# Gathering the tokens' expert rows in two rounds, with four additions placed in the last up projection

## The reference, cut to what matters

```python
def moe(x, gate_w, w1, w3, w2):            # x: 1024 x 512, E = 8, F = 1024, TOPK = 2
    logits = x @ gate_w
    topv, topi = top_k(logits, 2)
    probs = softmax(topv)
    for e in range(8):
        g = silu(x @ w1[e]) * (x @ w3[e])
        out += w[:, e:e + 1] * (g @ w2[e])   # w: probs at the token's two experts, else 0
    return out

out = h + moe(rmsnorm(h), ...)
x = layernorm(x + out)
```

## Time and profile before

| | |
|---|---|
| timed runs, us | 1427.38, 1428.01, 1431.57 |
| profiled execution, us | 1442.2 |
| its span, first to last instruction | 1440.6 |
| mean granted clock of TensorE | 0.965 |
| PE busy | 1318.8 us, 92% |
| DVE busy | 1023.2 us, 71% |
| ACT busy | 808.7 us, 56% |
| POOL busy | 366.7 us, 25% |

### The profile page before, as it was taken

One profiled execution on the slowest core, in us unless ns is written; L12 is line 12 of the kernel. 1 busy time (PEld: TensorE's weight loads), 2 busy tenths in 40 slices (PEclk: granted clock), 3 DMA queues, 4 the chain that ended last, 5 costly groups with the idle time before them and its releaser, 6 DMA issues. The chain is left out here.

```text
span 1440.6 us, 24551 instructions
## 1 busy us (share of the span) xinstructions
PE 1318.8 (92%) x7925; PEld 713.0 (49%) x7925; DVE 1023.2 (71%) x1966; ACT 808.7 (56%) x1460; POOL 366.7 (25%) x602
## 2 busy tenths in 40 slices
PE   7988999999999999998688999999959999999974
PEld 4444444444444444443344555555436556666751
DVE  5847777777777777777567887888768556666736
ACT  5447666666666666666336575665734444555422
POOL 5402020202010101104256365664326000000042
PEclk9999999999999999999798999999979999999987
DMA  8327776666665767587453453535595866677641
GB/s 250 60 59 133 148 116 136 122 128 139 115 144 112 153 116 150 106 182 132 154 158 72 87 118 60 142 64 102 100 235 184 297 171 188 212 225 239 232 125 60
DMA packets 451868, 206.18 MB, mean 143 GB/s; under 512 B 401088, under 2 KB 415424, under 8 KB 451776
## 3 DMA queue, kind: packets, MB, share of 16 engines
q1 hardware_dynamic: 448640, 196.67, 58.1%
q0 software_dynamic: 2560, 8.39, 1.8%
q10 hardware_dynamic: 576, 0.00, 0.0%
HBM read 87.38 MB, written 16.45 MB: 72 GB/s over the span
## 5 line engine op out<-in xcount | busy, mean ns | idle before, releaser
L1539 DVE SCALAR_TENSOR_TENSOR X<-xa_SC,xa_rs,X 128x1024 f16<-128x1024 f32 x128 | 164.4, 1284 | 98.5 <-issue 97.8
L1347 ACT ACTIVATE X<-xa_SC,xa_rs 128x1024 f16<-128x1024 f32 x128 | 147.1, 1149 | 110.7 <-POOL xa_rs L1044 110.7
L1220 PE MATMUL xa_psS<-xa_KT,xa_QT 128*128 128x512 f16 x768 | 186.4, 379 | 6.1 <-DVE xa_mn L1572 4.7
L1232 PE MATMUL xa_psO<-wide,xa_V 128*128 128x512 f16 x768 | 173.3, 383 | 7.1 <-DMA wide<-X 7.0
L1044 POOL TENSOR_SCALAR xa_rs<-xa_rc,flag 128x1 f32<-128x1 f32 x128 | 34.2, 267 | 516.2 <-DVE xa_rc L1532 516.2
L1572 DVE CUSTOM_DVE_ANT_0 xa_SC<-xa_psS,maskb 128x1024 f32<-128x1024 f32 x128 | 155.1, 1211 | 4.5 <-PE xa_psS L1220 2.4
L1369 ACT ACTIVATE xa_SC<-xa_SC,xa_mn 128x1024 f32<-128x1024 f32 x128 | 145.4, 1136 | 13.4 <-DVE xa_mn L1572 13.3
L1232 PEld LDWEIGHTS xa_psO<-wide,xa_V 128*128 128x128 f16 x768 | 74.5, 98 | 102.1 <-issue 16.9
L1220 PEld LDWEIGHTS xa_psS<-xa_KT,xa_QT 128*128 128x128 f16 x768 | 73.4, 98 | 90.7 <-DVE xa_mn L1572 9.4
L1369 ACT ACTIVATE sa_SC<-sa_SC,sa_mn 128x128 f32<-128x128 f32 (+3 forms) x128 | 71.5, 559 | 78.2 <-DVE sa_mn L1572 78.0
L2065 PE MATMUL rmoe_psU<-rmoe_XGT,W 128*128 128x352 f16 (+6 forms) x768 | 109.4, 291 | 3.8 <-issue 3.8
(11 more groups left out here) (295 smaller groups left out, 2251.5 us busy)
## 6 DMA issues: line engine op xcount, KB each, us to landing
first<-in_L_ffn_w_dram SPq DMA_DIRECT2D x12, 2048.0 KB
W2raw<-in_L_ffn_w_dram SPq DMA_DIRECT2D x8, 2048.0 KB, 9.0
expert_rows_dram<-zeros SPq DMA_DIRECT2D x10, 512.0 KB, 9.5
xa_WPraw<-in_L_xattn_Wq_dram SPq DMA_DIRECT2D x8, 512.0 KB, 11.0
xa_WOraw<-in_L_xattn_Wo_dram SPq DMA_DIRECT2D x8, 512.0 KB, 4.6
first<-in_L_ffn_wq_dram SPq DMA_DIRECT2D x4, 1024.0 KB, 7.7
first<-in_L_ffn_wo_dram SPq DMA_DIRECT2D x4, 1024.0 KB, 5.9
first<-in_L_ffn_w_dram SPq DMA_DIRECT2D x8, 512.0 KB, 4.5
```

What stands on the lines that cost most here:

```text
L1220: last = nc.tensor.matmul(psS[j % NSC][:, c:c + cw], QT[b][:, hq, g, t * P:(t + 1) * P], KT[b][:, hk, c:c + cw], start=(q == 0), stop=(q = ...
L1232: last = nc.tensor.matmul(psO[:, c:], V[b][:, hv, blk, :], PT[g % NPT][:, blk, hp, c:], start=(blk + q == 0), stop=(blk == NBLK - 1 and q ...
L1347: nc.scalar.activation(PN[j % NPN][:, 0:w // P, 0, :], by_block(SC[j % NSC], w), ACT.Identity, scale=rs[:, j % 4:j % 4 + 1]).then_inc(norm ...
L1539: nc.vector.scalar_tensor_tensor(out=PN[j % NPN][:, 0:w // P, 1, :], in0=by_block(SC[j % NSC], w), scalar=rs[:, j % 4:j % 4 + 1], in1=PN[j ...
```

## The change

The rows are fetched in two rounds. In the early round every token fetches its two rows, one transfer at a time, as soon as the stores of places 0 to 4 have landed; a row that is of place 5, 6 or 7 is replaced by the new row 0, which is zero. In the second round, behind all stores of places 0 to 6, the 16 gathers are issued again into the same tiles with row numbers from which those of places 0 to 4 are made too large by adding 8192, and place 7's are past the bound as they are: a bounds check leaves them out, and what was fetched before stays. Four of the sixteen additions move: each of f=4 to f=7 of place 7's up projection has one (tile 0, k=0 and 1; tile 1, k=0 and 1). The others stand as: tiles 2, 3, 4; L2224; tiles 5, 6, 7; L2224; finish 0 to 7. Three small DVE operations make the row numbers. All first rows move by one.

```diff
--- before.py
+++ after.py
@@ -32,12 +32,14 @@
 CAP = 352
 CTL = -(-CAP // P)
 CAPS = (352, 352, 336, 304, 288, 272, 256, 240)
-FIRST_ROW = tuple(sum(CAPS[:p]) for p in range(E))
+FIRST_ROW = tuple(1 + sum(CAPS[:p]) for p in range(E))
 TILES = tuple(-(-c // P) for c in CAPS)
 TILES_BEFORE = tuple(sum(TILES[:p]) for p in range(E + 1))
-ROWS = sum(CAPS)
+ROWS = 1 + sum(CAPS)
 PINNED = 16384.0
 LAST = E - 1
+LATE = E - 3
+OUTSIDE = 8192.0
 PAIRS = ((0, 0), (0, 1), (1, 0))
 
 
@@ -1877,6 +1879,9 @@
         first_bank = psT + psY
         slots = sb("slots", [P, 2, NT], U32)
         slotf = sb("slotf", [P, 2, NT], F32)
+        below = sb("below", [P, 2, NT], F32)
+        early_row = sb("early_row", [P, 2, NT], U32)
+        late_row = sb("late_row", [P, 2, NT], U32)
         part = sb("part", [P, 2, NT, E], F32)
         highest = sb("highest", [P, NT], F32)
         last_at = sb("last_at", [P, NT], F32)
@@ -1910,6 +1915,7 @@
         down_ready, y_copied = sem("down_ready"), sem("y_copied")
         y_stored = [sem(f"y_stored{r}") for r in range(CTL)]
         gathered = [sem(f"gathered{t}") for t in range(NT)]
+        early_in, rows_named = sem("early_in"), sem("rows_named")
         chosen_done, y_hi, y_lo, part_ready = sem("chosen_done"), sem("y_hi"), sem("y_lo"), sem("part_ready")
         spread_in = [sem(f"spread_in{t}") for t in range(NT)]
         negm_done, shift_done = sem("negm_done"), sem("shift_done")
@@ -2025,17 +2031,25 @@
             pool.wait_ge(pad_zeroed, 2)
             nc.gpsimd.memset(half[:], -0.5).then_inc(half_done, 1)
             pool.wait_ge(half_done, 1)
-            pool.wait_ge(up_ready, LAST * FC + FC // 2)
+            pool.wait_ge(rows_named, 2)
+            pool.wait_ge(scattered, 16 * 2 * NT)
+            for r in range(CTL):
+                pool.wait_ge(y_stored[r], 16 * sum(TILES[p] > r for p in range(LATE)))
+            for t in range(NT):
+                for k, dst in enumerate((Y1, Y2)):
+                    if t + k:
+                        pool.wait_ge(early_in, 16 * (2 * t + k))
+                    pool.indirect_dma_start(out=dst[:, t, :], out_offset=None, in_=YG[0:FIRST_ROW[LATE], :],
+                                            in_offset=bass.IndirectOffsetOnAxis(ap=early_row[:, k, t:t + 1], axis=0)
+                                            ).then_inc(early_in, 16)
+            pool.wait_ge(early_in, 16 * 2 * NT)
             for r in range(CTL):
                 pool.wait_ge(y_stored[r], 16 * sum(TILES[p] > r for p in range(LAST)))
-            pool.wait_ge(scattered, 16 * 2 * NT)
             for t in range(NT):
-                if t >= 2:
-                    pool.wait_ge(gathered[t - 2], 32)
                 for k, dst in enumerate((Y1, Y2)):
-                    pool.indirect_dma_start(out=dst[:, t, :], out_offset=None, in_=YG[0:ROWS, :],
-                                            in_offset=bass.IndirectOffsetOnAxis(ap=slots[:, k, t:t + 1], axis=0)
-                                            ).then_inc(gathered[t], 16)
+                    pool.indirect_dma_start(out=dst[:, t, :], out_offset=None, in_=YG[0:FIRST_ROW[LAST], :],
+                                            in_offset=bass.IndirectOffsetOnAxis(ap=late_row[:, k, t:t + 1], axis=0),
+                                            bounds_check=FIRST_ROW[LAST] - 1, oob_is_err=False).then_inc(gathered[t], 16)
             for i in range(NT):
                 pool.wait_ge(mv_done, i + 1)
                 nc.gpsimd.tensor_scalar(ve[:, i:i + 1], mv[:, i, 1:2], EPS, 1.0, ALU.add, ALU.mult).then_inc(ve_done, 1)
@@ -2209,6 +2223,8 @@
                     if first and f < NT // 2:
                         for t in range(2 * f, 2 * f + 2):
                             nc.vector.tensor_tensor(X[:, t, :], X[:, t, :], X2[:, t, :], ALU.add).then_inc(x_added, 1)
+                    if last and f >= FC // 2:
+                        combine(f // 2 - 2, f % 2)
                     if p in choose_at and f < len(choose_at[p]):
                         if choose_at[p][f] == 0:
                             dve.wait_ge(scattered, 16 * 2 * NT)
@@ -2216,7 +2232,7 @@
                         nc.vector.tensor_scalar(chosen[:, t, :], row1[:], last_at[:, t:t + 1], None,
                                                 ALU.is_equal).then_inc(chosen_done, 1)
                 if last:
-                    for t in range(3):
+                    for t in range(2, 5):
                         combine(t)
                 for r in range(TILES[p]):
                     if last:
@@ -2224,7 +2240,7 @@
                         nc.vector.tensor_tensor(YH[0:width(p, r), r, 1, :], psY[r % 2][0:width(p, r), :],
                                                 YH[0:width(p, r), r, 0, :], ALU.subtract).then_inc(y_lo, 1)
                         if r == 0:
-                            for t in range(3, 6):
+                            for t in range(5, 8):
                                 combine(t)
                         else:
                             finish_rows(r - 1)
@@ -2299,10 +2315,12 @@
             chained(nc.vector.scalar_tensor_tensor(out=last_part[:], in0=slotf[:], scalar=last_row, in1=p12[:],
                                                    op0=ALU.is_ge, op1=ALU.mult))
             chained(nc.vector.tensor_tensor(last_wt[:], last_part[:, 0, :], last_part[:, 1, :], ALU.add))
+            chained(nc.vector.tensor_scalar(below[:], slotf[:], float(FIRST_ROW[LATE]), None, ALU.is_lt))
+            nc.vector.tensor_tensor(early_row[:], slotf[:], below[:], ALU.mult).then_inc(rows_named, 1)
+            nc.vector.scalar_tensor_tensor(out=late_row[:], in0=below[:], scalar=OUTSIDE, in1=slotf[:],
+                                           op0=ALU.mult, op1=ALU.add).then_inc(rows_named, 1)
             over_experts(dve, step)
             for t in range(TILES[LAST] - 1, NT):
-                if t + 5 < NT:
-                    combine(t + 5)
                 finish_rows(t)
 
 
@@ -2486,9 +2504,7 @@
         xg = XG.rearrange("(n p r) d -> n p r d", p=P, r=2)
         cleared = [(xg[i], zeros[:].unsqueeze(1).broadcast_to([P, 2, D]), zeroed) for i in range(-(-ROWS // (2 * P)))]
 
-        for r in range(TILES[LAST]):
-            at, w = FIRST_ROW[LAST] + r * P, min(P, CAPS[LAST] - r * P)
-            cleared.append((YG[at:at + w, :], zeros[0:w, :], zeroed))
+        cleared.append((YG[0:1, :], zeros[0:1, :], zeroed))
 
         X2 = sb("X2", [P, NT, D], F32)[:]
         wide = sb("wide", [P, 2, NT, D], F32)[:]
```

## The result

The changed kernel took 1443.53 us (median of 4 runs, 1441.47 to 1446.67) beside 1427.7 for the kernel before (4 runs, 1426.81 to 1431.57): a ratio of 1.0107 (95% interval 1.0083 to 1.0132). It is slower by 15.8 us; the forecast was 1425.8 with a range up to 1436.

The account below looks back on a forecast made before the run. It took DVE's order from 1403.9 on as the bound, without the profiled stall. +0.86 for the second L2224, -3.04 for two addition pairs and 0 gave -2.2: 1428.0 - 2.2 = 1425.8, range 1420 to 1436.

Parts of the forecast that it names:

- The choice on which most hung: Taking the 1384 to 1401 standstill as mostly absent from timed runs, and working from the order without it.
- the stall: In place 7, ScalarE stands still 14.38 us during the gathers and DVE waits; removing it makes everything 14.9 us earlier.
- the rebuilt 1427.3: Profiled time of before, 1442.2, less 14.9 us for the stall; set beside timed 1427.38 and 1428.01.
- the stall is in the timed runs too: Rival: a thin second gather round removes it, giving 1411; stall real, in part or whole, chance 0.16.
- Part 2: Sixteen early gathers on POOL from 1304, one at a time: 3.6 us each free, 5.0 beside loads, bounds 3.6 and 7.3.
- S: Time at which POOL's second gather round can begin: 1375.3 forecast, bounds 1371.8 and 1386.5.
- Part 3: Second round's sixteen issues, 1.27 us apart, 19.3 in all; tile 0 needs S <= 1376.7, tile 7 S <= 1375.9.
- the early round ends too late: Rival: early gathers delay the second round, net S - 1378.1, giving 1433 to 1442; chance 0.24.
- Part 1: Four DVE additions moved into place 7's up projection, three hidden at no cost: net 2.2 us off.
- the second low half: DVE's second L2224, a subtraction for the last place's rows: 1399.5 before without the stall, forecast 1400.35 after.
- What they hinder: Early gathers beside place 6's weight loads, which have 8 us of slack: cost 0, bounds 0 and 3.
- The DVE port: DVE holding the port pair shared with GpSimd lengthens some five early periods by up to 0.9; S 1379 at most.

Follow-up runs that it names:

- series 3 and 6: Two series of kernels timed one after the other on one chip; the unchanged kernel before, timed between them, had medians of 1429.67 and 1428.99 us.
- e12: Changed kernel with the early round for places 0 to 3 instead of 0 to 4: 1427.08 us beside 1429.67 for the kernel before, ratio 0.9984.
- e1: Changed kernel with the waits between the sixteen early gathers taken out: 1455.2 us, ratio 1.0097 to the kernel before at 1443.0.
- e7: Changed kernel loading only 16 of 1024 columns of w1 and w3 of places 6 and 7: 1440.96 us.
- e16: Same program as e12, timed in another series: 1446.6 us beside 1444.43 for the kernel before, ratio 1.0016.
- e6: Changed kernel whose early rows of places 5 to 7 are replaced by a row of their own instead of row 0: 1443.17 us.
- e2: Changed kernel with all sixteen additions back in the order of before, both gather rounds kept: 1442.48 us, ratio 0.9995 to the kernel before.
- e8: Kernel before without the hold at f=3, each group of four gathers waiting for the landing of the one before: 1431.09 us beside 1443.94, ratio 0.9913.
- e15: Same kernel as e8, timed in another series: 1428.91 us beside 1444.43 for the kernel before, ratio 0.9897.
- e9: e8 with four additions moved into the up projection and the later order fitted: 1428.49 us beside 1429.67 for the kernel before, ratio 0.9988.
- e18: Same kernel as e9, timed in another series: 1427.88 us beside 1428.99 for the kernel before, ratio 0.9992.
- e13: Kernel before, unchanged, run for its profile: 1445.58 us.

## Why the prediction was wrong

**The choice on which most hung held, in part by luck.** I took the stall for absent in the timed runs. The 46 runs of before in series 3 and 6, at 1429.7 and 1429.0, are 2 us from the rebuilt 1427.3; in e12 even a round without pauses ran without a stall. My reason, that the profiled execution has the stall and the timed ones don't, was wrong: it is there or not for whole series of timed runs, and the times that I had were of the lower level. The rival "the stall is in the timed runs too" (1411) held for its condition in four series and failed in its mechanism: before is at 1443 to 1444 there and the change still at 1443.9 to 1446.8. A thin second round doesn't take the stall away (e1, e7 and e16 stall in theirs); a late one was without it, and costs as much.

**The step that failed is Part 2, "I take 5.0, between 3.6 and 7.3".** The six gathers beside loads had 7.55 on average (6.10 to 8.61), so the scatter's 7.3 was the nearest row, and the argument that a gather alone is nearer the free value, since it shares with one stream only, was wrong. With 7.55 for the loaded 49 us and the 4.0 that the free ones took (not 3.6) for the other 18, 11.0 gathers are over at 1371, not 14.8, and five more at the 3.87 that they took from 1370.24 on give 1390.3; measured 1389.58. The loaded period alone takes S from 1375.3 to 1387.2, and the free one, 4.0 for 3.6, adds the rest. My upper bound, 1386.5, had nearly the right loaded period but kept 3.6 for the free ones. e7 shows the cause (loads), e6 excludes another (many reads of row 0), and e12 shows the long periods without the stall.

**Part 3.** The sixteen issues took 21.77 from first to last, 2.4 more than the 19.3 of the sum, and the last landed 2.64 behind its issue, not 3.6: DVE had tile 7 at 1414.01, S + 24.4 instead of S + 22.9 (my formula for the tiles gives 22.65 there). The bound S <= 1375.9 for tile 7 held in kind: e12, with S at 1373.65, had no wait for a tile.

**The rival "the early round ends too late"** is what happened: "at 5.5 it is S = 1392 and 1442". With S = 1389.58 its S - 1378.1 gives +11.5, 1439.5; measured 1441.5 in the profile and 1443.5 in the median. Of the 4 us that are left, 1.5 are the last tile of Part 3; the others are open. It had a chance of 0.24 and should have had more than the forecast, given the only loaded row that there was.

**Part 1.** -2.2 for the four additions: e12, with lateness and stall both absent, is 2.6 below its before, ratio 0.9984, interval 0.9968 to 1.0, in agreement, though the interval reaches to no change; the better support is the second low half within 0.1 of its forecast place. On a late second round they are worth nothing (e2).

**What they hinder.** Cost 0 held: TensorE had no gap from 1304 to 1384.

**The DVE port.** The issues of 1326.16 and 1334.77 took 1.94 and 1.89 instead of 0.95, near the 0.9 more that the prediction had as its bound (whose five times 0.9 make S 1379.8, not 1379). More of it is in the second round: in e12 an issue takes 1.0 to 1.3 up to 1388.66 and 1.4 to 1.5 from 1389.97 on, when DVE's additions run back to back (1389.86 on), and in e16, the same program, where DVE stands still for most of the round, 1.00 to 1.02 throughout, a pitch of 1.31. So of the 1.45 some 0.14 go with DVE's work and 0.04 are left for the bounds check over the 1.27 of before. The Trainium skill's "SBUF — State Buffer", section on the two sides of SBUF, describes an exclusive hold of the port pair that DVE shares with GpSimd; the traces agree with it.

## What to carry to other kernels

An indirect transfer that is waited for before the next one is issued costs what the loads beside it make it cost: take its period from a row in which it runs beside such loads (7.3 was there), not from one between, and multiply by the number in the chain before asking what it saves. Before moving something in front of a wait, work out the latest start from which the move still pays (here 1378), and compare it with the worst row. Bursts of indirect transfers were worth breaking by pauses here: four and a wait for their landing gave 13 to 15.5 us where there was a stall (e8, e15). Where there was none they ran only together with the four additions, 1.2 and 1.1 us below before (e9, e18), so that what the pauses alone cost there is not shown; little room is left for it beside the 2.2 of the additions.

## What the runs showed that was not expected

One program has two times, 1.0 to 1.4% apart, that hold for a whole series: the kernel before at 1443 to 1444 in four series and at 1429 to 1430 in two, e12 and e16 at 1427.1 and 1446.6. In the upper one TensorE, ScalarE and DVE stand still or get one to three instructions at a time, which costs the kernel before 14 to 15 us, in the stretch in which POOL issues indirect transfers without a pause, at a DMA share of 0.25 and also with most rows left out. It does not appear where four transfers and a landing alternate, nor in any of the four profiles of the changed kernel, whose early round has a wait behind each transfer and whose second round lies where TensorE is waiting for tile 0 and in the down projection, nor in e2.

The cause isn't settled. An engine that runs out of instructions would look like this. The Trainium skill's "Runtime: NRT & Kernel Launch", section "Instruction fetch mechanics", says that sequencers fetch their instructions by DMA and that this is mostly hidden; in the stalled series it would then not be hidden. But the records of the instruction queues show no difference: 44 and 48 packets in the stalled e16 and e13, 44 and 47 in e12, and in e13 one arrives at 1391 to 1392 while TensorE stays starved until 1404.5. What makes a series stall or not, and how long a burst may be, stays open.
